# Routed gated activations turned by VectorE through memory instead of by TensorE

## The chip, the cores and the metric

The kernel runs on one core of one Trainium2 chip. The metric is the device time of one execution in microseconds (us); lower is better. The engines are TensorE (PE; its weight loads are listed apart as PEld), VectorE (DVE), ScalarE (ACT), GpSimd (POOL) and SyncE (SP), which only issues DMAs here. ACT and POOL issue DMAs too. Each engine runs its own instruction stream in order, and the streams meet at semaphores.

## The reference

A pre-norm transformer layer on x of shape (2, 2048, 512), all in float32. First attention, then a feed-forward part with eight routed experts (two chosen per token) and one shared expert:

```python
x = x + attn(layernorm(x), ...)              # 8 heads, causal
x = x + ffn(layernorm(x), ...)

scores = sigmoid(xt @ gate_w.T)              # ffn: xt is (4096, 512)
top_scores, top_idx = top_k(scores, 2)       # normalised, times 2.5
combine = sum(one_hot(top_idx, 8) * top_scores[..., None], axis=1)
h = einsum('td,edh->eth', xt, w1)            # w1, w3: (8, 512, 352)
u = einsum('td,edh->eth', xt, w3)
y = einsum('eth,ehd->etd', silu(h) * u, w2)  # w2: (8, 352, 512)
routed = einsum('etd,te->td', y, combine)
shared = silu(xt @ sw1) * (xt @ sw3) @ sw2
out = routed + shared
```

The kernel computes an expert only for the tokens that chose it.

## The kernel before, in words

The kernel has three stages: projections and attention (to about 610 us), the shared expert with the routing (32 tiles of 128 tokens, to about 950 us), and the routed experts (to the end). The change touches the routed stage alone.

There the (token, expert) pairs have been sorted by expert into `NB` = 71 blocks of 128 rows. Block n goes through this pipeline; numbers are lines of the kernel before:

- POOL gathers the block's 128 normalised rows out of memory in four indirect DMAs (`gather`, L659), two blocks ahead.
- DVE turns them to feature-major (`turn`, L1209): the rows come in quarters, so that 32x32 block transposes by DVE give the 128x128 transpose that the product needs.
- PE makes the two up products (`up`, L1046): 2 x 4 float32 products of 352 columns, 16 matmul instructions in the trace, into banks 1 to 4.
- ACT takes silu of the first (L831), DVE multiplies by the second (`gated`, L1320), giving `act_sb`, 128 rows by 352.
- PE turns `act_sb` in three 128x128 transposes (`at`, L1029) into bank 5, and ACT copies them to `act_t` (`at_copy`, L809).
- PE makes the down product (`down`, L1057): 3 products of 512 columns, 6 matmul instructions, into bank 6.
- DVE scales by the routing weight (`y`, L1337), and POOL adds the rows into the output by an indirect DMA with add (`scatter`, L669). Each scatter waits until the one before has landed.

Each engine's stream is written step by step by `step(n, k)`; `run_steps` unrolls the first u steps, puts the middle in a loop of u steps, and unrolls the rest. In step n PE does at(n-1), up(n), down(n-1); ACT at_copy(n-1), silu(n); DVE turn(n+1), the row numbers of block n+3 (L1309 to L1313), gated(n), y(n-1); POOL gather(n+2), scatter(n-2). PE reads the block's expert number into a register ahead of each product (L1061). Double buffers exist of `xq`, `xg_t`, `act_sb`, `act_t`, `y_sb` and the up banks; `silu` and bank 6 are single, so down(n) waits for y(n-1). SP loads the blocks' row lists (L613). `s_` names and `ro[...]` are semaphores of the routed stage; `ss` stands for the shared or the routed set.

Of the kernel before, what the change touches and what calls it, by code (L numbers as in the profile page):

```python
# [11 lines left out]
E, H = 8, 352  # L12
TOP_K, ROUTED_SCALE = 2, 2.5
P = 128
# [7 lines left out]
HC = -(-H // P)  # L22
HP = HC * P
HL = H - (HC - 1) * P
# [5 lines left out]
NB = TOP_K * T // P + E - 1  # L30
# [16 lines left out]
QP = 4  # L47
# [165 lines left out]
def program(nc, io):  # L213
    ctx = ExitStack()
    with ctx:
# [7 lines left out]
        attn_rows = dram("attn_rows", [T, C])  # L223
        xn2_rows = dram("xn2_rows", [T + P, D])
        table = dram("table", [TABLE, 2])


        const = sb("const", [P, CONST_W])
# [77 lines left out]
        xg_t = sb("xg_t", [P, 2, DC, P])  # L306

        xq = sb("xq", [P, 2, QP, DC, QW])
        silu = sb("silu", [P, H])
        act_sb = sb("act_sb", [P, 2, HP])  # L310
        act_t = sb("act_t", [P, 2, HC, P])
# [87 lines left out]
        s_xns = [sem(f"xn2_stored_{i}") for i in range(2)]  # L399
        s_lg, s_sig = sem("logits_ready"), sem("sigmoid_ready")  # L400
        s_r = sem("route_chain")
        s_sel, s_cnt, s_cntr = sem("selected_ready"), sem("ranks_ready"), sem("ranks_read")
        s_slot = sem("slots_ready")
        s_table, s_put = sem("table_filled_with_spare_rows"), sem("pairs_stored")
# [215 lines left out]
        def _(pool):  # L620
# [59 lines left out]
            for n in range(NB):  # L680
                if n < NB - 2:
                    gather(n + 2)
                if n >= 2:
                    scatter(n - 2)
            scatter(NB - 2)
            scatter(NB - 1)
            for i in range(2):
                pool.wait_ge(ro[f"stored_{i}"], 16 * ((NB + 1 - i) // 2))

# [1 line left out]
        def _(act):  # L691
# [111 lines left out]
            def experts(ss, count, u):  # L803
                def at_copy(n, k):
                    act.wait_ge(ss["at"], n + 1)

                    if k >= 2:
                        act.wait_ge(ss["dn"], n - 1)
                    nc.scalar.copy(act_t[:, k % 2], psum[:, 5, 0:HP].rearrange("p (c n) -> p c n", c=HC)).then_inc(ss["ate"], 1)  # L809

                def to_copy(n, k):
                    act.wait_ge(s_to, n + 1)

                    if k >= 2:
                        act.wait_ge(s_op, n - 1)
                    nc.scalar.copy(attn_t[:, k % 2, :], psum[:, 0, HP:]).then_inc(s_toe, 1)

                def step(n, k):
                    if ss is sh and k < count - 3:
                        to_copy(n + 3, k + 3)  # L820
                    if k >= 1:
                        at_copy(n - 1, k - 1)
                    if ss is sh:
                        for t0, m in GROUPS:
                            if n == t0 + m:
                                scores_of(t0, m)
                    act.wait_ge(ss["up"], n + 1)

                    if k >= 1:
                        act.wait_ge(ss["a"], n)  # L830
                    nc.scalar.activation(silu[:, :], psum[:, 1 + k % 2, 0:H], ACT.Silu).then_inc(ss["silu"], 1)  # L831

                if ss is sh:
                    for n in range(count):
                        step(n, n)
                    scores_of(*GROUPS[-1])
                else:
                    run_steps(act, count, step, u)
                at_copy(count - 1, count - 1)

            def scores_of(t0, m):
                act.wait_ge(s_lg, t0 + m)
                nc.scalar.activation(logits[:, t0:t0 + m, :], logits[:, t0:t0 + m, :], ACT.Sigmoid).then_inc(s_sig, 1)

            experts(sh, NT, XR)
            experts(ro, NB, 2)

        @block.tensor
        def _(pe):
# [152 lines left out]
            def experts(ss, count, shared, u):  # L1002
# [60 lines left out]
                def step(n, k):  # L1063
                    if shared and n in COUNT_AT:
                        ranks(COUNT_AT[n], min(n + 3, NT))
                    if shared and k < count - 2:
                        front(n + 2, k + 2)
                    if shared and k < count - 3:
                        turn(n + 3, k + 3)
                    if k >= 1:  # L1070
                        at(n - 1, k - 1)
                    up(n, k, expert(n))
                    if k >= 1:
                        down(n - 1, k - 1, expert(n - 1))

                if shared:
                    pe.wait_ge(s_x1, 2)
# [1 line left out]
                        step(n, n)  # L1079
                else:  # L1080
                    run_steps(pe, count, step, u)
                at(count - 1, count - 1)
                if shared:
                    ranks(len(GROUPS) - 1, NT)
                down(count - 1, count - 1, expert(count - 1))

# [18 lines left out]

            pe.wait_ge(s_idx, 1)
            pe.wait_ge(s_w, 16 * 4 * E)
            experts(ro, NB, False, 2)

        @block.vector  # L1110
        def _(dve):
# [181 lines left out]
            def experts(ss, count, shared, u):  # L1293
# [21 lines left out]
                def gated(n, k):  # L1315
                    dve.wait_ge(ss["silu"], n + 1)

                    if k >= 2:
                        dve.wait_ge(ss["at"], n - 1)
                    nc.vector.tensor_tensor(act_sb[:, k % 2, 0:H], psum[:, 3 + k % 2, 0:H], silu[:, :], ALU.mult).then_inc(ss["a"], 1)  # L1320
                    if shared:
                        nc.vector.tensor_copy(logits[:, bass.ds(n, 1), :].rearrange("p a e -> p (a e)"),
                                              psum[:, 1 + k % 2, H:H + E]).then_inc(s_lg, 1)

                def y(n, k):
                    dve.wait_ge(ss["dn"], n + 1)
# [14 lines left out]
                def step(n, k):  # L1341
# [9 lines left out]
                    if shared:  # L1351
                        if k < count - 1:
                            turn(n + 1, k + 1)
                        for g, part in CHOOSE.get(n, ()):
                            choose(g, part)
                    if k >= 1:
                        y(n - 1, k - 1)

                if shared:
                    for n in range(count):  # L1360
# [4 lines left out]
                else:  # L1365
                    for k in range(3):
                        row_numbers(k, k)
                    turn(0, 0)
                    run_steps(dve, count, step, u)
                y(count - 1, count - 1)  # L1370

            r_at = [0]
# [103 lines left out]
```

## Time and profile before

| | |
|---|---|
| median of 3 runs | 1536.67 us (1536.3 to 1538.73) |
| the profiled execution's own time | 1535.9 us |
| its span, first to last instruction | 1534.0 us |
| PE busy | 1414.4 us, 92% |
| DVE, ACT, POOL busy | 893.3, 508.8, 452.3 us |
| mean granted TensorE clock | 0.965 of full |

The span runs from the first to the last instruction of the core. Busy shares are means over three stages that have different limits, so a change in the routed stage is read in the routed stage, from about 950 us on: which engine has no gap there, and what each of the others waits for. A matmul's end is modelled, so small overlaps between matmul groups are no error; the chain of waits cuts them into pieces that add up.

### The profile page before, as it was taken

The page shows a single profiled execution, that of the slowest core. Times are in us where ns is not written, and L with a number is a line of the kernel's source. Part 1 is how long each engine was busy: PE and PEld are TensorE (multiplying, and loading weights), DVE is VectorE, ACT ScalarE, POOL GpSimd, SP SyncE. Part 2 cuts the span into 40 slices and gives each one's busy share as a digit, 9 for nine tenths or more (in the row PEclk, how much of TensorE's full clock was granted, in tenths as well). Part 3 has the DMA queues.
Part 4 walks back from the last instruction along what each step waited for, and adds up shares of the span by engine and source line. Part 5 has one row for each costly group of instructions (what it writes and reads, how often), then busy time and mean ns, then how long its engine had stood idle before and what let it go on. Part 6 is the DMA issues. An engine that isn't in the chain of part 4 may idle for free.

```text
span 1534.0 us, 21932 instructions
## 1 busy us (share of the span) xinstructions
PE 1414.4 (92%) x6059; PEld 704.4 (46%) x6060; DVE 893.3 (58%) x2655; ACT 508.8 (33%) x1042; POOL 452.3 (29%) x431
## 2 busy tenths in 40 slices
PE   6997999999999998899899984699999999999996
PEld 3552223333433332455455542355555555555553
DVE  4898998888788861678687864233333333333331
ACT  4662456766676677212021121011111111111110
POOL 0000000000000000000222252667777777777771
PEclk9996999999999999899899997799999999999998
DMA  7685310310320000466676752244444444444442
GB/s 219 217 237 156 80 39 4 78 43 5 68 58 4 5 5 16 135 195 180 158 174 176 180 101 50 48 67 71 69 69 69 69 69 69 69 70 70 69 69 35
DMA packets 124854, 136.81 MB, mean 89 GB/s; under 512 B 37046, under 2 KB 86590, under 8 KB 124774
## 3 DMA queue, kind: packets, MB, share of 16 engines
q1 hardware_dynamic: 101350, 96.56, 24.4%
q0 software_dynamic: 21520, 37.84, 14.4%
q10 hardware_dynamic: 1904, 1.46, 0.3%
q8 instruction: 36, 0.59, 0.2%
q14 instruction: 44, 0.36, 0.1%
HBM read 87.03 MB, written 48.83 MB: 89 GB/s over the span
## 4 chain that ended last, share of the span: by engine, by line
PE 72%; DVE 13%; DMA 5%; issue 5%; ACT 2%; SPq 1%; POOL 1%; ACTq 0%; DVEq 0%; POOLq 0%
PE psum L1046 28%; PE psum L1057 14%; PE psum L959 8%; PE psum L941 7%; PE psum L923 6%; PE psum L873 3%; DVE arena L1239 3%; DVE psum L1237 2%; PE psum L1029 2%; DMA xq<-xn_rows 2%; DMA xn_rows<-xg 2%; DMA attn_cur<-attn_rows 1%; PE psum L1020 1%; PE psum L944 1%; ACT arena L709 1%
## 5 line engine op out<-in xcount | busy, mean ns | idle before, releaser
L1046 PE MATMUL psum<-arena,xg_t 128*128 (+2 forms) x1648 | 520.1, 470 | 20.5 <-DVE xg_t L1209 19.9
L1046 PEld LDWEIGHTS psum<-arena,xg_t 128*128 128x128 f32 x1648 | 312.4, 195 | 182.8 <-issue 32.9
L781 ACT ACTIVATE arena<-psum 128x512 f32<-128x512 f32 (+3 forms) x640 | 303.6, 535 | 176.2 <-PE psum L941 87.3
L643 POOL DMA_INDIRECT table<-const,slot_i x64 | 62.5, 976 | 865.2 <-DVE slot_i L1424 756.1
L659 POOL DMA_INDIRECT xq<-xn_rows,quad_rows x284 | 272.2, 958 | 96.4 <-issue 88.9
L1057 PE MATMUL psum<-arena,act_t 128*128 (+3 forms) x618 | 282.5, 593 | 1.2 <-ACT act_t L809 0.7
L1239 DVE TENSOR_REDUCE arena<-psum 128x1 f32<-128x512 f32 x384 | 251.0, 685 | 30.5 <-PE psum L923 29.9
L923 PE MATMUL psum<-arena 96*128 96x512 bf16 (+3 forms) x640 | 219.1, 363 | 17.8 <-DVE arena L1237 9.6
L1320 DVE TENSOR_TENSOR act_sb<-psum,silu 128x352 f32<-128x352 f32 x103 | 54.0, 524 | 284.8 <-ACT silu L831 226.9
L941 PE MATMUL psum<-arena 99*128 99x512 bf16 (+3 forms) x640 | 215.0, 353 | 3.5 <-ACT arena L781 2.7
L831 ACT ACTIVATE silu<-psum 128x352 f32<-128x352 f32 x103 | 47.8, 464 | 466.8 <-PE psum L1046 410.5
L1057 PEld LDWEIGHTS psum<-arena,act_t 128*128 128x128 f32 (+1 forms) x618 | 117.5, 190 | 121.4 <-issue 100.0
L959 PE MATMUL psum<-arena 128*32 128x512 f32 (+3 forms) x1280 | 150.7, 543 | 3.8 <-ACT arena L792 2.3
L669 POOL DMA_INDIRECT out_rows<-y_sb,row_i x71 | 114.4, 1612 | 91.0 <-issue 65.6
L1237 DVE CUSTOM_DVE_ANT_0 psum<-psum,constb 128x128 f32<-128x128 f32 (+3 forms) x256 | 123.9, 499 | 20.2 <-PE psum L923 19.7
L941 PEld LDWEIGHTS psum<-arena 99*128 99x128 bf16 x640 | 61.3, 97 | 154.3 <-ACT arena L781 112.6
L1337 DVE TENSOR_SCALAR y_sb<-psum,block_pair 128x512 f32<-128x512 f32 x71 | 53.3, 751 | 118.1 <-PE psum L1057 116.5
L809 ACT COPY act_t<-psum 128x384 f32<-128x384 f32 x103 | 49.4, 479 | 203.5 <-PE psum L1057 105.6
L923 PEld LDWEIGHTS psum<-arena 96*128 96x128 bf16 x640 | 62.4, 99 | 106.0 <-DVE arena L1239 41.9
L873 PE MATMUL psum<-arena 128*128 128x512 f32 x192 | 84.7, 597 | 0.0
L1209 DVE STREAM_TRANSPOSE xg_t<-xq 128x512 f32<-128x512 f32 x103 | 72.3, 702 | 19.9 <-DMA xq<-xn_rows 13.4
L1029 PEld LDWEIGHTS psum<-const,act_sb 128*128 128x128 f32 x309 | 39.9, 143 | 53.5 <-issue 52.8
(138 smaller groups left out, 894.6 us busy)
## 6 DMA issues: line engine op xcount, KB each, us to landing
arena<-qk_parts SPq DMA_DIRECT2D x48, 256.0 KB, 6.2
arena<-in_w SPq DMA_DIRECT2D x16, 704.0 KB
arena<-in_x SPq DMA_DIRECT2D x32, 256.0 KB, 4.4
x<-in_x SPq DMA_DIRECT2D x32, 256.0 KB
xn_rows<-xg SPq DMA_DIRECT2D x32, 256.0 KB
xq<-xn_rows SPq DMA_DIRECT2D x128, 64.0 KB
out_rows<-y_sb SPq DMA_DIRECT2D x32, 256.0 KB
qk_parts<-arena SPq DMA_DIRECT2D x16, 384.0 KB, 3.2
```

The source lines that it names most:

```text
L659: nc.gpsimd.indirect_dma_start(out=xq[:, n % 2, g].rearrange("p c b -> p (c b)"), out_offset=None, in_=quarters, in_offset=bass.IndirectOf ...
L669: nc.gpsimd.indirect_dma_start(out=io["out"][:, :], out_offset=bass.IndirectOffsetOnAxis(ap=row_i[:, n:n + 1], axis=0), in_=y_sb[:, n % 2, ...
L781: nc.scalar.activation(probs[:, at_b % PS, d * P:], psum[:, NA + at_b % NBK, 0:CH - d * P], ACT.Exp, scale=float(HD) ** -0.5).then_inc(s_e, 1)
L873: i = nc.tensor.matmul(psum[:, bank, :], w_t[:, which, c, :], xn_t[:, c, :], start=c == 0, stop=c == DC - 1)
L923: ins = nc.tensor.matmul(psum[:, bank, 0:w], stack_q[g][0:KR, j, qt * P:(qt + 1) * P], stack_k[g][0:KR, j, k0:k0 + w], start=True, stop=True)
L941: ins = nc.tensor.matmul(psum[:, bank, 0:CH - d * P], stack_k[g][0:KM, j, kt * P:(kt + 1) * P], stack_q[g][0:KM, j, c * CH + d * P:(c + 1) ...
L959: ins = nc.tensor.matmul(psum[VW * j:VW * (j + 1), 6, d * P:], v_sb[g][:, kt, j, :], probs[:, (at_pv * G + j) % PS, d * P:], start=kt == 0 ...
L1046: i = nc.tensor.matmul(psum[:, bank + k % 2, 0:w], xg_t[:, k % 2, c, :], rhs, start=c == 0, stop=c == DC - 1)
L1057: i = nc.tensor.matmul(psum[:, 6, :], act_t[0:r, k % 2, c, :], rhs, start=c == 0, stop=c == HC - 1)
L1209: nc.vector.transpose(xg_t[:, k % 2].rearrange("p c (g a) -> p g c a", g=QP), xq[:, k % 2]).then_inc(done, 1)
L1237: ins = nc.vector.tensor_tensor_reduce(scores, scores, cbf("mask")[:, CH - w:], 1.0, NEG, ALU.add, ALU.max, top_of)
L1239: ins = nc.vector.tensor_reduce(top_of, scores, AX.X, ALU.max)
```

## The change

PE's three transposes per routed block and ACT's copy of them go. Instead DVE writes the gated activations in an order of four quarters of 96, ACT stores them to a buffer in memory (`act_rows`, two blocks of 128 x 384 floats, 192 KB each) by one DMA, and loads them again by four DMAs, one per group of 32 partitions, into `aq`, a view of the buffer `xg` that the shared stage no longer uses. DVE then transposes 32x32 blocks from `aq` to `act_t`. ACT loads block n-1 after it has stored block n; DVE turns block n-2 in step n; PE's down product and DVE's y stand at n-3, and POOL's scatter at n-4. PE's and ACT's loops hold four steps instead of two. The shared stage keeps its transposes.

```diff
@@ gpsimd
-                if n >= 2:
-                    scatter(n - 2)
-            scatter(NB - 2)
-            scatter(NB - 1)
+                if n >= 4:
+                    scatter(n - 4)
+            for n in range(NB - 4, NB):
+                scatter(n)
@@ scalar
+                def store_gated(n, k):
+                    act.wait_ge(ss["a"], n + 1)
+                    if k >= 2:
+                        act.wait_ge(s_aq[k % 2], QP * used(n, k))
+                    act.dma_start(act_rows[k % 2], act_sb[:, k % 2, :]).then_inc(s_as[k % 2], 16)
+                def load_gated(n, k):
+                    act.wait_ge(s_as[k % 2], used(n, k) + 16)
+                    if k >= 2:
+                        act.wait_ge(ss["ate"], n - 1)
+                    w = HP // QP
+                    for i in range(QP):
+                        act.dma_start(aq[i * QW:(i + 1) * QW, k % 2],
+                                      act_rows[k % 2][:, i * w:(i + 1) * w].rearrange("(g a) d -> a g d", g=QP)).then_inc(s_aq[k % 2], 16)
@@ scalar, step: after silu(n)
-                    if k >= 1:
+                    if ss is sh and k >= 1:
                         at_copy(n - 1, k - 1)
...
+                    if ss is ro:
+                        store_gated(n, k)
+                        if k >= 1:
+                            load_gated(n - 1, k - 1)
...
-            experts(ro, NB, 2)
+            experts(ro, NB, 4)
@@ tensor, step
-                    if k >= 1:
+                    if shared and k >= 1:
                         at(n - 1, k - 1)
                     up(n, k, expert(n))
-                    if k >= 1:
-                        down(n - 1, k - 1, expert(n - 1))
+                    behind = 1 if shared else 3
+                    if k >= behind:
+                        down(n - behind, k - behind, expert(n - behind))
...
+                    for n in range(count - 3, count - 1):
+                        down(n, n, expert(n))
...
-            experts(ro, NB, False, 2)
+            experts(ro, NB, False, 4)
@@ vector, gated: the routed form
+                        if k >= 2:
+                            dve.wait_ge(s_as[k % 2], used(n, k))
+                        place = act_sb[:, k % 2, :].rearrange("p (i c b) -> p c i b", i=QP, c=HC)
+                        whole = (HC - 1) * P
+                        by_chunk = lambda a, c: a.rearrange("p (c i b) -> p c i b", c=c, b=QW)
+                        nc.vector.tensor_tensor(place[:, 0:HC - 1], by_chunk(psum[:, 3 + k % 2, 0:whole], HC - 1),
+                                                by_chunk(silu[:, 0:whole], HC - 1), ALU.mult)
+                        nc.vector.tensor_tensor(place[:, HC - 1, 0:HL // QW], psum[:, 3 + k % 2, whole:H].rearrange("p (i b) -> p i b", b=QW),
+                                                silu[:, whole:H].rearrange("p (i b) -> p i b", b=QW), ALU.mult).then_inc(ss["a"], 1)
...
+                def turn_gated(n, k):
+                    dve.wait_ge(s_aq[k % 2], QP * (used(n, k) + 16))
+                    if k >= 2:
+                        dve.wait_ge(ss["dn"], n - 1)
+                    nc.vector.transpose(act_t[:, k % 2].rearrange("p c (g a) -> p g c a", g=QP),
+                                        aq[:, k % 2].rearrange("p g (c b) -> p g c b", c=HC)).then_inc(ss["ate"], 1)
@@ vector, step: after gated(n)
-                    if k >= 1:
+                    if shared and k >= 1:
                         y(n - 1, k - 1)
+                    if not shared and k >= 2:
+                        turn_gated(n - 2, k - 2)
+                    if not shared and k >= 3:
+                        y(n - 3, k - 3)
...
                     run_steps(dve, count, step, u)
+                    turn_gated(count - 2, count - 2)
+                    y(count - 3, count - 3)
+                    turn_gated(count - 1, count - 1)
+                    y(count - 2, count - 2)
```

On PE, this is the head of the loop before: the three transposes of block n-1, then the expert number, then the up product of block n (`routed_a` is the gated activations' semaphore, `routed_ate` that of `act_t`, `routed_xte` that of the turned rows).

```order
L113 UNCONDITIONAL_BRANCH
L113 ISA
L1026 REGISTER_ALU [waits routed_a]
L1029 MATMUL psum<-const,act_sb 128x128 [waits routed_ate]
L1029 MATMUL psum<-const,act_sb 128x128 x2
L1061 ISA
L1061 TENSOR_LOAD eid_i
L1061 ISA x2
L1033 REGISTER_ALU
L1046 ISA [waits routed_a,routed_xte]
L1046 MATMUL psum<-arena,xg_t 128x352
```

And the same place in the changed kernel:

```order
L113 UNCONDITIONAL_BRANCH
L113 ISA
L1086 TENSOR_LOAD eid_i
L1086 ISA x2
L1058 REGISTER_ALU
L1061 REGISTER_ALU [waits routed_xte]
L1071 ISA [waits routed_a]
L1071 MATMUL psum<-arena,xg_t 128x352
```

The transposes are gone and the up product stands straight behind the down product of the step before; its wait for the gated activations is the one of block n-2, for the bank.

On ACT, the routed stage of the kernel before begins like this, silu and copies in turn:

```order
L831 ACTIVATE silu<-psum 128x352 [waits routed_up]
L809 COPY act_t<-psum 128x384 [waits routed_at]
L831 ACTIVATE silu<-psum 128x352 [waits routed_a,routed_up]
```

In the changed kernel the beginning is this (`gated_rows_stored` tells that a store has landed, `gated_quarters_loaded` that the loads have):

```order
L851 ACTIVATE silu<-psum 128x352 [waits routed_up]
L827 DMA act_rows<-act_sb 128x384 [waits routed_a]
L851 ACTIVATE silu<-psum 128x352 [waits routed_a,routed_up]
L827 DMA act_rows<-act_sb 128x384 [waits routed_a]
L835 DMA xg<-act_rows 32x4x96 [waits gated_rows_stored_0]
L835 DMA xg<-act_rows 32x4x96 x3
L851 ACTIVATE silu<-psum 128x352 [waits routed_a,routed_up]
L827 DMA act_rows<-act_sb 128x384 [waits gated_quarters_loaded_0,routed_a]
L835 DMA xg<-act_rows 32x4x96 [waits gated_rows_stored_1]
L835 DMA xg<-act_rows 32x4x96 x3
```

Five DMA issues have come between two silus, the first of them behind a wait for DVE's product of the same block.

## Rows read from the trace of the kernel before

**Rows 1.** Busy time by engine and stage; PE, PEld, DVE, ACT, POOL, then clock.

```profile
1100.00:1200.00 100.00, 100.00 (x329) 58.45 (x328) 31.05 (x91) 12.26 (x26) 71.53 (x66) 1.00 0.43 69
```

**Rows 2.** Chain that ended last, one steady block (start us, us, what).

```profile
1201.16 2.58 PE psum L1057 x6
1203.74 0.33 PE psum L1029 x3
1204.07 4.74 PE psum L1046 x16
```

**Rows 3.** Timeline of the same block, DVE, ACT and POOL (start, us, engine).

```profile
1201.20 0.46 ACT L831 ACTIVATE silu<-psum 128x352 f32<-128x352 f32 x1 [4.18 <-PE psum L1046]
1201.69 0.53 DVE L1320 TENSOR_TENSOR act_sb<-psum,silu 128x352 f32<-128x352 f32 x1 [3.29 <-ACT silu L831]
1203.91 0.75 DVE L1337 TENSOR_SCALAR y_sb<-psum,block_pair 128x512 f32<-128x512 f32 x1 [1.69 <-PE psum L1057]
1204.58 0.70 DVE L1209 STREAM_TRANSPOSE xg_t<-xq 128x512 f32<-128x512 f32 x1
1204.94 1.62 POOL L669 DMA_INDIRECT out_rows<-y_sb,row_i  x1 [0.97 <-issue]
1206.87 1.00 POOL L659 DMA_INDIRECT xq<-xn_rows,quad_rows  x1 [0.30 <-issue]
```

**Rows 4.** L1061, PE's reads of the expert number (x, min/median/max ns).

```profile
L1061 PEldq TENSOR_LOAD <-eid_i x142: 296/302/494, 951.0 to 1515.7; - x142
```

**Rows 5.** Issues of DMAs, ACT's L694 and SP's L488 (min/median/max ns).

```profile
L694 ACTq DMA_DIRECT2D arena<-in_wq x2: 552/583/614, 0.7 to 1.3; - x2
L488 SPq DMA_DIRECT2D xq<-xn_rows x128: 303/432/1673, 613.7 to 920.0; - x128
```

**Rows 6.** Chain in the shared stage: a DMA load under traffic.

```profile
892.36 6.86 DMA xq<-xn_rows
```

**Rows 7.** DMA queues, 1100 to 1500 us (packets, MB, share of 16 engines).

```profile
q0 software_dynamic: 14287, 27.54, 40.6%
q1 hardware_dynamic: 9216, 0.21, 1.4%
```

**Rows 8.** DMA queue of SP in the shared stage, 750 to 850 us.

```profile
q1 hardware_dynamic: 15915, 17.69, 69.9%
```

**Rows 9.** Window after the scatter of 1204.94; last columns clock, DMA share, GB/s.

```profile
1208.60:1209.10 0.50, 0.50 (x3) 0.22 (x2) 0.00 (x0) 0.26 (x1) 0.50 (x1) 1.00 0.94 162
```

**Rows 10.** Chain at the start of the routed stage.

```profile
966.04 6.58 PE psum L1046 x16
972.62 6.51 issue
979.12 0.90 PE psum L1029 x3
980.02 6.35 PE psum L1046 x16
...
1005.34 4.74 PE psum L1046 x16
```

**Rows 11.** Timeline there, ACT and DVE.

```profile
978.05 0.46 ACT L831 ACTIVATE silu<-psum 128x352 f32<-128x352 f32 x1 [35.64 <-remote]
978.99 0.70 DVE L1209 STREAM_TRANSPOSE xg_t<-xq 128x512 f32<-128x512 f32 x1
```

**Rows 12.** Chain at the end of the program.

```profile
1509.80 4.74 PE psum L1046 x16
1514.54 2.59 PE psum L1057 x6
...
1517.15 0.76 DVE y_sb L1337
...
1518.18 4.64 DMA out_rows<-y_sb,row_i
...
1523.88 1.54 POOL out_rows L669
```

More of the change, by code:

```diff
@@ L225, in program @@
         table = dram("table", [TABLE, 2])
+        act_rows = dram("act_rows", [2, P, HP])
         const = sb("const", [P, CONST_W])
@@ L308, in program @@
         xq = sb("xq", [P, 2, QP, DC, QW])
+        aq = xg[:, :, 0:HP].rearrange("p k (g n) -> p k g n", g=QP)
         silu = sb("silu", [P, H])
@@ L401, in program @@
         s_r = sem("route_chain")
+        s_as = [sem(f"gated_rows_stored_{i}") for i in range(2)]
+        s_aq = [sem(f"gated_quarters_loaded_{i}") for i in range(2)]
         s_sel, s_cnt, s_cntr = sem("selected_ready"), sem("ranks_ready"), sem("ranks_read")
@@ L836, in experts @@
                     scores_of(*GROUPS[-1])
+                    at_copy(count - 1, count - 1)
                 else:
                     run_steps(act, count, step, u)
-                at_copy(count - 1, count - 1)
+                    load_gated(count - 1, count - 1)
             def scores_of(t0, m):
@@ L1081, in experts @@
                     run_steps(pe, count, step, u)
-                at(count - 1, count - 1)
+                    for n in range(count - 3, count - 1):
+                        down(n, n, expert(n))
                 if shared:
+                    at(count - 1, count - 1)
                     ranks(len(GROUPS) - 1, NT)
@@ L1316, in gated @@
                     dve.wait_ge(ss["silu"], n + 1)
-                    if k >= 2:
+                    if shared and k >= 2:
                         dve.wait_ge(ss["at"], n - 1)
-                    nc.vector.tensor_tensor(act_sb[:, k % 2, 0:H], psum[:, 3 + k % 2, 0:H], silu[:, :], ALU.mult).then_inc(ss["a"], 1)
+                    if shared:
+                        nc.vector.tensor_tensor(act_sb[:, k % 2, 0:H], psum[:, 3 + k % 2, 0:H], silu[:, :], ALU.mult).then_inc(ss["a"], 1)
+                    else:
+                        if k >= 2:
[7 more added lines that the diff above has]
+                                                silu[:, whole:H].rearrange("p (i b) -> p i b", b=QW), ALU.mult).then_inc(ss["a"], 1)
                     if shared:
```

## The prediction

> **What bounds the kernel now.** I read the busy windows by stage first, then the chain of waits, then the timeline of one block, then the DMA queues. In the routed stage PE has no gap: 100 us busy in 100 us at the full clock, with DVE at 31%, ACT at 12% and POOL at 72% [rows 1]. The chain of waits consists of PE alone there, with a period of 4.74 + 2.58 + 0.33 = 7.65 us: up product, down product, three transposes [rows 2]. From the fifth up product, at 1005.34 [rows 10], to the last, at 1509.80 [rows 12], there are 66 periods: 504.46 / 66 = 7.643 us each. So what counts is what PE does per block, provided that nothing else has a period above PE's new one, and what happens at the two ends.
>
> **The steady part.** PE loses the transposes, 0.33 us per block [rows 2], and gains nothing. New period if PE stays the bound: 7.643 - 0.33 = 7.31 us; I take 7.32 = 4.74 + 2.58. Below, it could be some 0.05 less, if the joints between groups vanish. Above, what could fill the gap on PE is the read of the expert number, 0.30 us [rows 4], now with no transposes to cover it: 7.62. It stands ahead of the down product already, with only matmuls in flight as cover, and the pieces of the chain join there without a gap (4.74 us from 1204.07 ends where the next group began) [rows 2]; so I take 0.
>
> What has to stay under 7.32 us:
>
> DVE: product in two pieces. 352 columns take 0.53 us in one; a second instruction adds its fixed part, at most one 0.53 more [rows 3]. I take 0.7 for both. The new transpose is 384 columns beside 512 in 0.70: between 0.53 and 0.70, I take 0.57. DVE goes from 31% of 7.64 = 2.4 us per block [rows 1] to 2.4 + 0.17 + 0.57 = 3.1. Lateness counts more than load. Let up(n) end at 0. In the kernel before silu starts 0.2 later and the product 0.7 later (silu 1201.20, product 1201.69) [rows 3]; the product of two pieces ends at 1.4, the turn of block n-2 at 2.0 if its data is there, and PE asks for that turn only at 2.58 + 4.74 = 7.32 (down(n-2) stands behind down(n-3) and up(n+1)). y(n-3) still follows its down product, which ends at 2.58. Hidden, with 5.3 us to spare.
>
> ACT: the copy goes (its place was between silus), five DMA issues come. ACT's own cost 0.58 us each at the start, SP's 0.43 [rows 5]: with 0.6, ACT does silu 0.46, waits for the product, then issues for 3.0 us, so it is free at 1.4 + 3.0 = 4.4 and next wanted at 7.3. Behind the waiting store stand only the loads and the next silu. It decides from (7.3 - 1.4) / 5 = 1.2 us an issue.
>
> The round through memory: store issued at 1.4. It has until ACT comes to the loads of this block, a period later and behind the next store, at 7.32 + 2.0 = 9.3. The loads are issued by 11.7, and DVE wants them at 14.64 + 1.4 = 16.0. If they are late, DVE stands, with y(n-1) and the next row turn behind; PE is reached only when turn (0.57) and y (0.75, and 0.25 to be seen) end after 21.96, where down(n) begins: with data that lands after 20.4. So 7.9 us are allowed to the store and 8.7 to the loads before PE notices, against 6.86 for a load in the loaded shared stage [rows 6].
>
> The DMA engines: in the steady part they are 42% busy [rows 7]: 0.42 x 16 x 7.643 = 51 us of engine time per block. The change adds 128 packets of 1536 B and 512 of 384 B. In the shared stage a packet of 1.1 KB takes 0.699 x 1600 / 15915 = 70 ns [rows 8]; a packet of the row lists, under 32 B, takes 0.014 x 6400 / 9216 = 10 ns [rows 7]. On a line between them, 384 B come to 31 ns and 1536 B to 95: 28 us, or 1.75 us on 16 engines. At 70 ns for every packet it is 45 us. The share becomes 68% (at most 82%). Hidden, but it lengthens landings.
>
> The Trainium skill speaks against this (DMA: Bandwidth & Descriptors, Specifications): under 512 B an engine reads, modifies and writes, so full rate wants 512 B or more. The 10 ns packets of the row lists show no such fixed price for loads. If each 384 B packet cost two of the mean ones all the same, the result would be the rival "engines full" below.
>
> POOL: four gathers of 0.95 to 1.00 with 0.30 ahead of each, a scatter of 1.62, and a gap of 0.97 before it [rows 3]. In that gap it waits for y: y ends at 1204.66, the scatter starts 0.28 later. Without the wait, with 0.30, the sum is 3.85 + 1.20 + 1.62 + 0.30 = 6.97 us: under 7.32, by 0.35. If the whole 0.97 is POOL's own, its period is 7.64 and the steady part gains nothing. I take 6.97.
>
> The scatter's landing: each scatter waits for the one before. At the program's end, with nothing else moving, one follows the other after 1523.88 - 1518.18 = 5.70 us [rows 12]. In the steady part traffic fills the engines 3.7 us after the scatter's start [rows 9], so it is more than 5.70; it is less than 7.64, since POOL waits for y and not for it. I take 6.3, nearer to the row that shows it. It has 1.0 us to spare at 7.32.
>
> **The start.** Before, up(0) ends at 972.62 and PE then waits 6.51 us, since the transposes of block 0 need silu(0), which comes only at 978.05 [rows 10, 11]; what holds ACT there the trace doesn't say, and I leave it as it is. Now up(1) follows at once, to about 977.4. up(2) needs the turn of block 2, which stands behind gated(0) on DVE: 978.55 + 0.7, turn to 980.0. With part of it at the lower clock (up(1) took 6.35 before) up(2) ends at 985.6, up(3) at 990.4, down(0) at 993.0, and there up(4) starts: 12.3 us before its 1005.34. Of these, two down products are only put off (5.2 us); the rest, 7.1, is the wait of 6.51 and the transposes, less what up(2) now waits. If ACT is held longer, up to 6 us of it go.
>
> **The end.** Before, the last scatter starts 9.34 us after the last up product's end (1514.54 to 1523.88), and the span ends 10.12 after that [rows 12]. Now four down products are left there, each waiting for y of the one before through bank 6: 2.58 + 0.76 + 0.25 = 3.6 us apart. But the scatters are 5.70 apart and bind: 3.64 after up's end as before (1518.18), then 9.34, 15.04, 20.74. The round of the last block (product 1.4, store, four loads, turn) is over by 15 even with 6 us a landing, and y(70) by 20, so it hides. Price: +11.4 us.
>
> **Sum.** Span = 993.0 + 66 x T + 4.74 + 20.74 + 10.12 = 1028.6 + 66 T. With T = 7.32 it is 1511.7 us, 22.3 less than 1534.0: -21.3 in the steady part, -12.3 at the start, +11.4 at the end. The execution's own time is 1.9 above its span (1535.9), and the median 0.8 above that: 1514.
>
> **Rivals.** (1) POOL becomes the bound: its gap is partly its own, or its five calls get slower beside DVE's longer work. For it: POOL has the least room of all. Against: the scatter follows y by the same 0.28 where POOL had waited. T between 7.4 and 7.64: 1520 to 1536, by the formula and 2.7 on top.
>
> (2) Slower: the scatter's landing. If all the new traffic (1.75 us) stands ahead of each scatter's packets, one follows the other after 6.3 + 1.75 = 8.05 us; `y_sb` fills, y waits, PE waits at bank 6. T = 8.05 gives 1563. It makes the kernel slower from T = 7.66 on, a spacing 1.4 above my 6.3. Against: ACT's store and loads come 1 to 6 us after the scatter's start in turns, mostly beside its descriptor work, not ahead of its packets.
>
> (3) Slower: engines full, by the price of two mean packets for each of 384 B: 51 + 512 x 0.14 + 128 x 0.095 = 135 us, T = 8.4, 1586. (The rule of the Trainium skill above points this way.) Or ACT at its dearest issue, 1.67 us [rows 5]: T = 1.4 + 8.4 = 9.8, over 1670.
>
> (4) It gains more: the turn of block 2 is not held by ACT, or the scatters at the end land sooner: 1507.
>
> **Chances.** The forecast 0.70 (1508 to 1520), rival 1 0.14, rival 2 0.05, rival 3 0.04, rival 4 0.07. The range that holds 8 in 10 is 1506 to 1530. What a measurement can tell from no change is about 0.2%, 3 us. Rival 1 reaches into it at its upper end: faster 0.87, same 0.04, slower 0.09.
>
> **What would show it.** Right: steady up products 7.32 apart, PE at 100% in the windows, no L1029 in the routed stage, POOL's gap before the scatter down from 0.97 to about 0.6, up(4) near 993, four scatters 5.7 apart at the end, DMA share near 0.68. Wrong: gaps on PE before down (turn late) or before up (row turn late), ACT issues over 1.2 us, or scatters that follow a landing in the steady part.

## The result: 2% slower, and the profile after

| sitting | chip | late ends | kernel before, us | kernel, us, ratio to before with its 95% interval |
| --- | --- | --- | --- | --- |
| 1 | | yes | 1536.49 | changed kernel 1565.39, 1.021 [1.018, 1.024] |
| 2 | 1 | no | 1518.29 | two_banks 1498.22, 0.988 [0.985, 0.992]; no_round 1497.45, 0.986 [0.983, 0.989]; before_with_traffic 1517.87, 1.000 [0.999, 1.001]; one_list_dma 1496.14, 0.985 [0.983, 0.988] |
| 3 | 7 | yes | 1524.54 | after_2 (the changed kernel) 1560.22, 1.022 [1.017, 1.026]; late_y_2 1628.20, 1.064 [1.058, 1.070]; late_y_banks 1617.29, 1.059 [1.055, 1.064]; banks_and_list 1557.02, 1.020 [1.014, 1.026] |
| 4 | 4 | no | 1518.50 | no_round_2 1496.43, 0.985 [0.980, 0.989]; before_with_traffic_2 1517.16, 1.000 [0.997, 1.003]; one_load 1503.32, 0.988 [0.983, 0.993]; tiny_dmas 1497.51, 0.985 [0.981, 0.990] |
| 5 | 5 | yes | 1534.21 | after_3 (the changed kernel) 1554.83, 1.015 [1.012, 1.018]; no_round_3 1545.18, 1.009 [1.006, 1.012]; before_with_traffic_3 1528.88, 0.998 [0.995, 1.000] |
| 6 | 11 | no | 1524.19 | loop_of_two 1506.18, 0.989 [0.986, 0.993] |
| 7 | 4 | yes | 1524.64 | loop_of_two_2 1547.75, 1.016 [1.013, 1.018] |
| 8 | 12 | yes | 1525.47 | lists_by_scalar 1589.10, 1.043 [1.038, 1.048] |

A sitting is one set of runs on one chip; only kernels of one sitting are compared. (In the expectations a sitting is a call.) In sitting 1 three of the four times of the kernel before are those taken ahead of the prediction (1536.3 to 1538.73), the fourth is 1526.79, and the record names no chip; sittings 3 and 5 show the loss again. "Late ends" is the phenomenon this study turned on: whether an engine that waits for TensorE sees the end of a matmul group at once or, in the changed kernel, up to 7.8 us late (after_3). Chip 4 had none in sitting 4 and many in sitting 7. In no_round, one_load and tiny_dmas the routed part of the output is not the reference's.

The forecast was 1514.0 us (1506 to 1530); the changed kernel took 1565.39 (four runs, 1562.8 to 1567.5). Its profiled execution took 1562.8, with a span of 1561.0 and a mean clock of 0.957 (before 1534.0 and 0.965).

First the windows, after and with the columns of [rows 1]:

```profile
1100.00:1200.00 100.00, 91.02 (x267) 50.50 (x265) 35.36 (x110) 5.57 (x12) 65.41 (x60) 0.98 0.53 109
1200.00:1300.00 100.00, 95.48 (x269) 52.73 (x270) 37.17 (x116) 6.03 (x13) 67.24 (x62) 0.95 0.55 113
```

PE, 100 us busy in 100 before, now stands 5 to 9% of the time, no other engine has more than 69 us of 100, and the mean granted clock of these windows is 0.98 and 0.95 of full. The chain of waits after, at the places of [rows 2] and [rows 12]:

```profile
1000.86 4.73 PE psum L1071 x16
1005.60 2.58 PE psum L1082 x6
1008.17 4.74 PE psum L1071 x16
...
1200.03 4.53 PE psum L1082 x6
1204.56 4.73 PE psum L1071 x16
1209.30 2.58 PE psum L1082 x6
...
1525.62 4.74 PE psum L1071 x16
1530.36 2.59 PE psum L1082 x6
...
1534.01 4.86 DMA out_rows<-y_sb,row_i
...
1539.61 4.67 DMA out_rows<-y_sb,row_i
...
1550.75 1.54 POOL out_rows L673
```

Most blocks have the forecast period (1000.86 to 1008.17 is 7.31), but some down products take 4.53 instead of 2.58. The waits of PE and of VectorE (engine and what it waited for: us in total, times, longest), 1000 to 1480 us, say where PE stands:

```profile
PE psum L1082 <- DVE y_sb L1385: 31.8, 15, 2.7
...
DVE y_sb L1385 <- remote: 43.5, 15, 3.7
```

and the timeline of one such place shows how it comes about:

```profile
1022.74 4.90 PE L1071 MATMUL psum<-arena,xg_t 128*128 x16
...
1027.47 2.74 PE L1082 MATMUL psum<-arena,act_t 128*128 x6
...
1030.05 4.90 PE L1071 MATMUL psum<-arena,xg_t 128*128 x16
...
1035.05 0.46 ACT L851 ACTIVATE silu<-psum 128x352 f32<-128x352 f32 x1 [14.23 <-PE psum L1071]
1035.55 0.42 DVE L1357 TENSOR_TENSOR act_sb<-psum,silu 128x256 f32<-128x256 f32 x1 [9.81 <-ACT silu L851]
...
1036.54 0.71 DVE L1385 TENSOR_SCALAR y_sb<-psum,block_pair 128x512 f32<-128x512 f32 x1
...
1037.52 2.84 PE L1082 MATMUL psum<-arena,act_t 128*128 x6 [2.57 <-DVE y_sb L1385]
```

The up product ended at 1027.6 and the down product at 1030.2. ScalarE had issued its last load by 1023.9 and VectorE ended its last operation at 1025.7, and neither moved before 1035.05. The trace also records when semaphores are updated: the update that tells of the up product stands at 1035.03, 7.4 us after its end. Then the two engines catch up, y is done at 1037.3, and the next down product, which waits for y through bank 6, starts 2.57 us late. Behind 8 of the 15 such stops the clock is at its lower level (half) for part of the next down product, which then takes 4.3 to 4.5 us; stops of some 2.5 to 2.7 us stand on both sides. One place (the column after POOL's is the granted clock, 0.61):

```profile
1199.90:1203.30 3.40, 3.27 (x5) 1.50 (x6) 2.14 (x8) 0.46 (x1) 2.65 (x3) 0.61 0.70 111
1203.40:1208.00 4.60, 4.60 (x15) 2.61 (x14) 1.86 (x6) 0.00 (x0) 3.69 (x4) 0.93 0.74 180
```

To count late silus I took the time from the start of an up product's last matmul to the silu that waits for it, for all silus after 1000 us. It is 0.50 us in all 68 of the kernel before; in the changed kernel it is over 1.5 us in 38 of 66, up to 8.0. Not each of these is a late end: when one silu comes 7 us late, ScalarE still has that block's store and loads to issue when the next up product ends. Without the time that ScalarE was still issuing, 24 of the 66 are over 1.5 us: these are late ends proper. Below, the counts are of late silus, with the late ends proper in brackets. Where no end is late, the semaphore's update stands 0.01 us after the group's end (all up and down products of the kernel before and of two_banks from 1000 to 1480 us).

### The profile page after: what moved, and what is told of

Read it like the earlier page. It is cut to its first block, busy times and chain, and to the rows that moved or that the text cites. A ratio compares the mean times of both kernels' runs of the same rounds, so it can differ in the third digit from the quotient of the medians.

```text
span 1561.0 us, 21930 instructions
## 1 busy us (share of the span) xinstructions
PE 1409.5 (90%) x5846; PEld 686.7 (44%) x5847; DVE 931.3 (60%) x2797; ACT 474.7 (30%) x971; POOL 452.2 (29%) x431
## 4 chain that ended last, share of the span: by engine, by line
PE 56%; DVE 15%; issue 10%; another core or an unknown queue 7%; DMA 5%; ACT 3%; ACTq 2%; SPq 1%; DVEq 0%; POOL 0%; POOLq 0%
PE psum L1071 18%; PE psum L1082 10%; PE psum L984 8%; PE psum L966 6%; PE psum L948 6%; PE psum L898 3%; DVE arena L1267 3%; DVE psum L1265 2%; ACTq L835 2%; DMA xq<-xn_rows 1%; DMA xn_rows<-xg 1%; DMA out_rows<-y_sb,row_i 1%; DMA attn_cur<-attn_rows 1%; ACT silu L851 1%
## 5 line engine op out<-in xcount | busy, mean ns | idle before, releaser
L1071 PEld LDWEIGHTS psum<-arena,xg_t 128*128 128x128 f32 x1648 | 318.5, 195 | 223.6 <-issue 73.3
L1082 PE MATMUL psum<-arena,act_t 128*128 (+3 forms) x618 | 299.3, 622 | 35.4 <-DVE y_sb L1385 34.9
L1082 PEld LDWEIGHTS psum<-arena,act_t 128*128 128x128 f32 (+1 forms) x618 | 119.7, 197 | 169.3 <-issue 152.6
L1357 DVE TENSOR_TENSOR act_sb<-psum,silu 128x256 f32<-128x256 f32 x71 | 30.2, 425 | 256.7 <-ACT silu L851 189.0
L898 PEld LDWEIGHTS psum<-arena 128*128 128x128 f32 x192 | 36.1, 192 | 41.9 <-issue 40.7
L969 PE MATMUL psum<-constb 128*128 128x128 bf16 x256 | 53.8, 222 | 0.0
```

The source lines that it names most:

```text
L898: i = nc.tensor.matmul(psum[:, bank, :], w_t[:, which, c, :], xn_t[:, c, :], start=c == 0, stop=c == DC - 1)
L1071: i = nc.tensor.matmul(psum[:, bank + k % 2, 0:w], xg_t[:, k % 2, c, :], rhs, start=c == 0, stop=c == DC - 1)
L1082: i = nc.tensor.matmul(psum[:, 6, :], act_t[0:r, k % 2, c, :], rhs, start=c == 0, stop=c == HC - 1)
```

## The experiments

**First question: is it the single bank, and do the new DMAs bring the late ends?** The second bank, in two_banks:

```
+ bank = 6 if shared else 5 + k % 2
+ if not shared and k >= 2: pe.wait_ge(ss["ye"], n - 1)     (was: k >= 1, n)
```

> The changed kernel, with the down products alternating between two PSUM banks (6 and 5), so that down(n) waits for y(n-2) instead of y(n-1). Theory A (what costs the time is that the end of a matmul group reaches VectorE up to 6 us late in some blocks, and the single bank 6 turns this into a stall of PE): a y that is up to 6 us late has a whole period of 7.3 us to spare, so the 15 gaps of 1.4 to 3.2 us before the down product go, and with them the half clock behind them: 49 us less, 1512 to 1520 us. Theory B (PE is held by something else that the trace puts down to y, for instance the turned activations coming late): the gaps stay, 1558 to 1568 us.

no_round: `store_gated` and `load_gated` aren't called, and `gated` and `turn_gated` wait for no store and no load.

> The changed kernel without ScalarE's store and its four loads; VectorE turns what lies in its buffer (the routed part of the output is therefore not the reference's). The order of the work, the blocks behind and VectorE's instructions stay. Theory A (the late ends of matmul groups come from the added DMAs): no late ends in the steady part, period 7.32 us, 1510 to 1520 us. Theory B (they come from the order: three blocks behind, PE without the pause for transposes, or from VectorE's work): about 15 late blocks stay, 1555 to 1568 us.

before_with_traffic: the kernel before, with the store and loads behind its silu.

> The kernel before, to which ScalarE's store and four loads per block are added, into a buffer that nobody reads; transposes and the order of the work stay. Theory A (the added DMAs alone make the late ends): late ends in 10 to 20 blocks here too, which hold y and silu and so PE: 1560 to 1590 us. Theory B (the DMAs harm only together with the new order): within 5 us of the kernel before, 1533 to 1541 us. Theory C (the price is ScalarE's issuing time between silu and the copy for the transposes, 5 x 0.45 us per block): every block longer by the same amount, not some of them.

one_list_dma: in `load_pairs` the four `sp.dma_start` become one with a source broadcast over four groups.

> The changed kernel, with SyncE's four small DMAs of row numbers per block made one (same 128 packets, a source read four times; 16 semaphore increments instead of 64). Theory A1 (late ends come from the number of DMAs issued or finished at one time, by SyncE and ScalarE together): the 15 late blocks fall to 5 or fewer, 1515 to 1535 us. Theory A2 (they come from ScalarE's packets, whoever else issues): as the changed kernel, 1558 to 1568 us.

Sitting 2 had no late ends in any kernel, so three of these tell nothing of them; what they show is the forecast's own case. two_banks, windows and chain:

```profile
1100.00:1200.00 100.00, 100.00 (x301) 56.97 (x300) 40.38 (x122) 6.48 (x14) 74.11 (x70) 1.00 0.60 127
```

```profile
979.28 4.74 PE psum L1071 x16
984.02 2.58 PE psum L1085 x6
986.60 4.74 PE psum L1071 x16
...
1461.96 4.74 PE psum L1071 x16
```

PE is busy throughout at 7.31 us a block. I take it that the edits of two_banks and one_list_dma can shorten nothing on a PE that never stands, and let both stand for the changed kernel there; it was not itself run without late ends. In before_with_traffic, which takes the time of the kernel before (1.000) and has its chain, up(4) starts at 985.66 and up(70) at 1490.12:

```profile
985.66 4.44 PE psum L1074 x15
...
1490.12 4.74 PE psum L1074 x16
```

So from it to two_banks: start 979.28 - 985.66 = -6.4; 66 periods (482.68 against 504.46) -21.8; from up(70) to the end of the span 34.0 against 23.6, +10.5. Sum -17.7, the difference of the spans (1513.7 and 1496.0). The forecast had -12.3, -21.3 and +11.4. So the steady part is as forecast, and the start brings half of what was forecast.

**Second question: what does a late y cost?** late_y_2 puts one reduction of 6144 elements between `dve.wait_ge(ss["dn"], n + 1)` and y if `k % 4 == 0`; late_y_banks is that with two banks; banks_and_list has both edits of sitting 2.

> The changed kernel once more, unaltered, on whatever chip this call gets. On the chip of the last call the kernel before took 1518.3 us, against 1536.5 where the changed kernel was first timed, and no end of a matmul group was seen late in four kernels there. Theory A (the late ends belong to the first chip or its state, and the change only pays for them more than the kernel before): where the kernel before is near 1518, this one is at 1496 to 1500, ratio 0.984 to 0.988; on a chip with late ends, ratio 1.015 to 1.025. Theory B (the late ends come with this exact kernel, and one list DMA or a second bank took them away): ratio 1.015 to 1.025 on any chip.

> The changed kernel, in which VectorE does a reduction of 6144 elements (about 6.4 us) between the end of the down product and y, in one block of four (18 blocks): y is late by as much as a late end made it, on any chip. Theory A (a late y stalls PE through the single bank: y is done 7.4 us after the down product, PE is back there after 4.74): a gap of about 2.7 us before the down product in 17 or 18 blocks, +48 us, and a half clock of some us behind part of them, up to 2 us each: 45 to 85 us over the unaltered kernel of the same call. Theory B (a late y alone doesn't hold PE): under 10 us more.

> The same delay of 6.4 us before y in one block of four, with the down products alternating between two banks. Theory A: PE comes back to a bank 7.3 us later than before, so y has 4.6 us to spare even so, and no gap is left: within 5 us of the unaltered kernel of the same call. Theory B (VectorE's backlog holds PE in other ways, by the row turn or the product): 20 us or more over it.

> The changed kernel with both edits of the last call: two banks for the down product and one DMA for a block's row numbers. On a chip without late ends both change nothing in the steady part (PE is busy 100% there with either): 1494 to 1500 us where the kernel before takes 1518. On a chip with late ends it is the faster of all: the same 1.3% under the kernel before.

The changed kernel is 2.2% slower again. That doesn't tell theory A of after_2 from B, since this sitting had late ends: 34 of 66 silus (22). late_y_2 costs 68 us more, which is theory A in size, though by other parts: the 13 stops from 1000 to 1480 us are 3.0 to 5.7 us, not 2.7, since late ends add to the delay. The second bank failed me: late_y_banks is 57 us over the unaltered kernel where I had expected at most 5, and banks_and_list 3 under it where I had expected some 55. The waits of PE in late_y_2, late_y_banks and banks_and_list, 1000 to 1480 us:

```profile
PE psum L1082 <- DVE y_sb L1388: 60.9, 13, 5.7
```

```profile
PE psum L1085 <- DVE act_t L1373: 42.5, 12, 3.9
PE psum L1071 <- DVE xg_t L1240: 12.6, 13, 1.8
```

```profile
PE psum L1085 <- DVE act_t L1373: 26.6, 12, 2.8
```

With the second bank y holds PE no more, but the turned activations do. VectorE works one list in order, and a silu that comes 7 us late makes product, turn and row turn late together. Bank 6 is only the tightest of several joints. In the two late_y kernels the reduction does the same by itself: it keeps VectorE busy for 6.55 us, where a late end leaves it idle, so they price a late VectorE and not a late y alone.

**Third question: bytes, number of DMAs, or neither?** one_load issues one load of 512 packets of 384 B; tiny_dmas shortens every row to 32 B.

> The changed kernel without ScalarE's store and four loads once more (the routed output is not the reference's), for a chip on which ends of matmul groups are seen late (the chip of the last call was such a one, that of the first call was not). On such a chip: Theory A (the added DMAs bring the late ends): no group seen over 1 us late after 1000 us, ratio 0.983 to 0.988. Theory B (the order of the work or the longer loop of TensorE brings them): 20 or more late groups, ratio 1.01 to 1.025. On a chip without late ends both give 0.986 as before and nothing is told apart.

> The kernel before with ScalarE's store and loads into a buffer nobody reads, once more, for a chip with late ends. Theory A: 20 or more late groups in the routed stage, which this kernel pays for more dearly (y, silu and the transposes all stand a block behind): ratio 1.02 to 1.06. Theory B: none, ratio 0.998 to 1.002.

> The changed kernel with one load DMA of 512 packets of 384 B instead of four of 128 each (quarters land in other places than they should, so the routed output is not the reference's; bytes and packets are the same, the semaphore increments of the loads 16 instead of 64). Theory A1 (the number of DMAs that finish together makes the late ends): on a chip with late ends fewer than half of them, ratio under 1.005. Theory A2 (the bytes or packets make them): as the changed kernel, 1.015 to 1.025.

> The changed kernel with its five DMAs of ScalarE kept in number and in their semaphore increments, but each row 32 B long: 128 packets for the store, 32 for each load (the routed output is not the reference's). Theory A1 (number of DMAs): on a chip with late ends as the changed kernel, 1.015 to 1.025. Theory A2 (bytes or packets): few late ends, ratio under 0.995.

Sitting 4 had no late ends: that time is 0.50 us for every silu in the four kernels, and nothing is told apart but that all versions of the new order gain 1.2 to 1.6% there.

> The changed kernel, unaltered, as the control of this call. On a chip without late ends: the forecast of the prediction holds there, 22 us under the kernel before: ratio 0.983 to 0.988, PE 100% busy in the windows from 1000 to 1400 us. On a chip with late ends: ratio 1.015 to 1.025 as twice before.

> The changed kernel without ScalarE's store and loads (the routed output is not the reference's). On a chip with late ends: Theory A (the added DMAs bring them): none after 1000 us, ratio 0.983 to 0.988. Theory B (the order of the work or TensorE's longer loop brings them): over 20 late groups, ratio 1.01 to 1.025. On a chip without: 0.985 again, and nothing told apart.

> The kernel before with ScalarE's store and loads into a buffer nobody reads. On a chip with late ends: Theory A (the added DMAs bring them in any order of work): over 20 late groups in the routed stage, ratio 1.02 to 1.06. Theory B (only with the changed order): none, 0.998 to 1.002. On a chip without: 1.000 again.

This sitting decides whether the DMAs are needed. In one sitting, on one chip, a window and PE's waits (1000 to 1480 us) of after_3, the same two of no_round_3, and a window of before_with_traffic_3, which has no waits of PE there:

```profile
1100.00:1200.00 100.00, 95.84 (x281) 53.54 (x280) 36.31 (x113) 6.02 (x13) 69.32 (x65) 0.98 0.57 117
```

```profile
PE psum L1082 <- DVE y_sb L1385: 28.0, 16, 3.0
```

```profile
1100.00:1200.00 100.00, 95.45 (x281) 53.45 (x281) 36.79 (x114) 5.75 (x13) 69.14 (x65) 0.98 0.40 68
```

```profile
PE psum L1079 <- DVE y_sb L1378: 24.4, 20, 2.5
```

```profile
1100.00:1200.00 100.00, 100.00 (x329) 58.45 (x328) 31.04 (x91) 12.23 (x26) 71.19 (x66) 1.00 0.61 120
```

Late silus are 51 of 67 (36) in after_3, 23 of 65 (23) in no_round_3 and 0 of 68 in before_with_traffic_3. So the DMAs are not needed for late ends, and in the old order they bring none: my theory A fell, and theory B holds. But B is wider than the order: no_round_3 also lacks PE's transposes and gives VectorE a product in two pieces and a second turn, and no run tells these from the order. With the DMAs it is worse: after_3 is 9.7 us slower than no_round_3.

**Fourth question: what in the order?** loop_of_two writes four blocks out and then loops over two, on TensorE and ScalarE:

```
- run_steps(pe, count, step, u)
+ run_steps_after_four(pe, count, step)      (Fori(2, count // 2 - 1), two blocks in its body)
```

> The changed kernel whose TensorE and ScalarE loops hold two blocks each, as in the kernel before, instead of four (the first four blocks are written out); the order of the work is the same. On a chip with late ends: Theory L (the longer loops bring them): none in the steady part, ratio 0.983 to 0.990. Theory O (the order does: no transposes and nothing that ever holds TensorE's instruction stream): 20 or more late groups, ratio 1.01 to 1.025 as the changed kernel. On a chip without: 0.985, nothing told apart.

> The changed kernel with TensorE's and ScalarE's loops of two blocks, once more, for a chip with late ends (known by late updates between 850 and 990 us, which every kernel has there, the kernel before too). Theory L (the longer loops bring the late ends): none after 1000 us, ratio 0.983 to 0.990. Theory O (the order does): 20 or more late groups, ratio 1.01 to 1.025. On a chip without: 0.985 to 0.989, nothing told apart.

In sitting 6 (no late ends) it gains 1.1%; in sitting 7 it is 1.6% slower, with 41 of 67 silus late (27): theory O, the longer loops are not needed for late ends. lists_by_scalar moves `load_pairs` behind `load_gated` on ScalarE's queue, with one DMA a block.

> The changed kernel with the row lists (one DMA per block) read and issued by ScalarE behind its four loads instead of by SyncE, which does nothing in the routed stage. Where late ends are about (known by late updates at 850 to 990 us): Theory S (they need SyncE's register operations and issues beside TensorE's): fewer than 5 late groups after 1000 us, ratio 0.983 to 0.992. Theory T (TensorE's stream alone, or the sum of the traffic, is enough): 20 or more late groups, ratio 1.01 to 1.025. Where none are about: 0.984 to 0.989 and nothing told apart.

Theory T: with SyncE idle 48 of 66 silus are late (21). It is the slowest version but for the delayed ones, because VectorE now also waits for the lists, which stand behind ScalarE's late silus:

```profile
DVE quad_rows L1342 <- DMA block_quads<-table: 93.4, 30, 4.8
```

## Why the prediction was wrong, by its steps

**The step that failed** is the period: T = 7.32 us over 66 blocks. In the profiled execution up(4) starts at 993.38 and up(70) at 1525.62: 532.24 / 66 = 8.06, and 66 x (8.06 - 7.32) = 49 us is the whole miss (1561.0 - 1511.7 = 49.3). It is made of the waits for y and of down products at the lower clock. Between the ends of up(3) and up(70) PE stands 32.1 us in the changed kernel and 0.3 in two_banks; its down products take 187.7 us there against 170.3, its up products 312.7 against 312.5. That is 31.8 + 17.4 + 0.2 = 49.4 us. The page shows the same: L1082 has a mean of 622 ns, against 593 in two_banks.

```profile
L1082 PE MATMUL psum<-arena,act_t 128*128 (+3 forms) x618 | 299.3, 622 | 35.4 <-DVE y_sb L1385 34.9
```

The prediction wrote that y(n-3) "still follows its down product, which ends at 2.58. Hidden, with 5.3 us to spare". It took the 0.2 us from a group's end to its reader, read off one block [rows 3], for a constant. That held for every block after 1000 us of the kernel before, and in sitting 5 for the old order beside the new one; in sittings with late ends it did not hold for the new order. The 5.3 us were also the slack of the turn and not of y. Through bank 6, y has what is left of the up product between two down products: 4.74 less 0.2, 0.75 and 0.25, some 3.5 us. And y(n-3) stands behind the product of block n in VectorE's list, so a silu 7.4 us late holds it, too: in the place at 1035.05 that is what made PE stand. And there was a sign: silu(0) at 978.05 [rows 11], 5.4 us after up(0) ended at 972.62 [rows 10]. The prediction noted that the trace doesn't say what holds ScalarE, and left it as a peculiarity of the start. It was a late end: in the trace of the kernel before, the semaphore's update for up(0) stands 5.4 us after the product's end. before_with_traffic, where no end is late, has no such wait: there up(0) ends at 960.58 and silu(0) follows at once.

```profile
953.91 6.67 PE L1074 MATMUL psum<-arena,xg_t 128*128 x16 [19.72 <-DVE xg_t L1237]
960.62 0.46 ACT L851 ACTIVATE silu<-psum 128x352 f32<-128x352 f32 x1 [30.18 <-PE psum L1074]
```

No rival stood for it. Rivals 1 to 3 were all about engines or landings, and each is refuted:

**POOL** (rival 1): in undisturbed blocks T is 7.31, and POOL's gap before the scatter is 0.43 to 0.87 us in two_banks from 1100 to 1150 us, mostly 0.65 (forecast 0.6, before 0.97 in [rows 3]). Its gap was a wait for y, as I took it.

**The scatter's landing** (rival 2): among POOL's waits from 1000 to 1500 none is for a landing; its scatter waits for y (73.0 us, 22 times). Rival 2's price, T = 8.05 and 1563 us, is met by the measured 8.06 and 1562.8 by chance: its mechanism is not what happened.

```profile
POOL out_rows L673 <- DVE y_sb L1385: 73.0, 22, 4.2
```

**Engines full, or dear issues** (rival 3): the DMA share is 0.53 to 0.58, 0.60 without late ends (forecast 0.68); ScalarE's queue takes 16.3% for 34569 packets in 400 us. By size, 24579 packets of 384 B took 24 ns in the mean (forecast 31), 6149 of 1536 B 67 ns (forecast 95), and 3841 of 4 B 9 ns. Per byte the short ones are dearer, 15.8 B per ns against 22.9, which is the way the rule of the Trainium skill points (DMA: Bandwidth & Descriptors, Specifications: under 512 B no full rate). The two mean packets for each of 384 B, 140 ns, that rival 3 made of it do not show. An issue takes 0.45 us in the median and 0.34 for the store, against the 0.6 I took.

```profile
q10 hardware_dynamic: 34569, 18.90, 16.3%
```

```profile
L835 ACTq DMA_DIRECT2D xg<-act_rows x284: 309/454/734, 982.7 to 1535.3; - x142
L827 ACTq DMA_DIRECT2D act_rows<-act_sb x71: 344/344/384, 972.9 to 1531.5; - x71
```

**Cheap parts right** (forecast in brackets): product in two pieces 0.42 + 0.25 (0.7), turn 0.57 (0.57), transposes' 0.33 gone from PE, and `turn_gated` waits 2.1 us in all for its loads from 1100 to 1500.

**Start and end:** up(4) starts at 993.38 (forecast 993.0), partly by luck, as the stage began 6.3 us earlier than before (959.72 against 966.04) and late ends took that back. From the end of up(70) to the end of the span it is 30.6 us (20.74 + 10.12 = 30.9), with scatters 5.4 to 5.7 apart at the end (5.7).

In sittings 2, 4 and 6, where the steady part is as forecast, all versions of the new order gain 1.1 to 1.6%, 15 to 22 us, of the 22 forecast. That some reach 22 is partly luck, since the start was forecast 5.9 us too good for such a sitting, and the one pair of spans worked out above differs by 17.7. In sittings 1, 3 and 5 the changed kernel loses 29, 36 and 21 us.

**What stays open** is what makes TensorE's ends late. Shown: they depend on something outside the kernel (no_round has none in sittings 2 and 4 and many in 5, loop_of_two none in 6 and many in 7), they need the new order or what comes with it in the steady part, more were counted with the added DMAs (36 against 23, one profiled execution each), and neither shorter loops, nor SyncE without its row lists, nor the second bank removes them. Argued only: in the kernel before, TensorE's instruction stream stops once a block for the product that its transposes need, and in the new order it runs ahead without ever stopping. late_y_2, where it is stopped in one block of four, has 1 late silu in 66, but late ys still. That a stop per block would cure it was not tried. Not tried either is a version without PE's reads of the expert number. Those reads, on TensorE's own stream, are slow in the traces that have late ends: from 1000 to 1480 us over 0.5 us in 39 of 117 in the changed kernel and in 51 of 123 in no_round_3, against none of 126 in the kernel before and in before_with_traffic_3, and 2 of 130 in two_banks. Whether that is a cause or another effect, no run tells.

```profile
L1061 PEldq TENSOR_LOAD <-eid_i x126: 296/302/313, 1003.7 to 1479.6; - x126
```

```profile
L1086 PEldq TENSOR_LOAD <-eid_i x118: 296/308/1322, 1000.0 to 1477.9; - x118
```

The first line is the kernel before, the second the changed kernel (minimum, median, maximum in ns).

## What to carry to other kernels

A bound read as "PE 100% busy, everything else hidden" holds for the hand-over times of that trace; before taking the slack away, ask what the joint costs if a hand-over takes 5 us once in three blocks, and look through the trace for a place where it already did. A wait that the trace doesn't explain, however far from the change, belongs to the forecast as a rival with a price. And measure a change on more than one chip and at more than one time when its gain is near 1%: here the same order of work was 1.5% faster or 2% slower.

## What the runs showed of the hardware

An end of a matmul group can reach the waiting engine up to 7.8 us late (the changed kernel, sitting 5), and 9.5 in late_y_banks, while ends of ScalarE and VectorE are seen at once: from 1000 to 1480 us VectorE's product starts 0.03 us after silu's end in all 51 blocks where it waited for it, and PE's down product 0.26 us after y's end at all 15 stops. In the same traces cheap operations of SyncE's stream take up to 0.7 us and more. The row lists' MOVE on SyncE (minimum, median, maximum in ns) in the changed kernel and in two_banks, without late ends:

```profile
L617 SPq MOVE block_quads<-table x284: 2/29/725, 948.0 to 1480.5; - x142
```

```profile
L617 SPq MOVE block_quads<-table x284: 29/29/43, 944.2 to 1415.1; - x142
```

A maximum of 725 ns against 43 is the quickest sign of such a sitting. The old order shows it there as well (699 ns in the kernel before, 708 in before_with_traffic_3), but only ahead of 1000 us. Since lists_by_scalar has late ends with SyncE idle, SyncE's slow operations are not their cause.

In the changed kernel 8 of PE's 15 stops, all of 2.2 to 2.6 us, were followed by a stretch at the lower clock: 4.53 us for a down product of 2.58, so a stop cost up to 1.95 us more than its own length. In late_y_2, behind stops of 3.0 to 5.7 us, the down products took 4.5 to 5.5 us.
